# Two edits at the tail of a convolution and attention kernel: the store of the last sample but one in three parts, and one product of the last sample moved behind the attention's products

## What is computed

```python
im = relu(x); mn = mean(im); p = clip(u.T @ (im - mn), -cv, cv)
q  = round((p - dmin) * scale) / scale + dmin      # dmin, dmax over all samples
y  = u @ q - mean(u @ q) + mn
```

```python
h = relu(bn(w_conv1 @ y)); d = relu(bn(w_dr @ h + b_dr))
cov = covariance of d over the 3136 pixels of the sample     # 128 x 128
r = rows of cov weighted with w_row, plus b_row
att = sigmoid(w_fc @ r + b_fc)
out = y * att
```

## Time and profile before

| what | value |
|---|---|
| time, median of 3 runs | 1894.13 us (1892.45 to 1895.07) |
| time of the profiled execution | 1892.99 us |
| its span | 1891.2 us |
| PE busy | 1672.6 us (88%) |
| DVE busy | 1536.7 us (81%) |
| ACT busy | 1488.9 us (79%) |
| DMA, mean over the span | 252 GB/s |

### The profile page before, as it was taken

The page is one execution under the profiler, slowest core; times in us unless marked ns, Lnnn a source line. Parts: engine busy times, 40 slices in busy tenths (PEclk is TensorE's granted clock), DMA queues, the critical chain, the costliest instruction groups (busy, mean ns, idle before and its releaser), DMA issues.

```text
span 1891.2 us, 39996 instructions
## 1 busy us (share of the span) xinstructions
PE 1672.6 (88%) x13394; PEld 1316.9 (70%) x13394; DVE 1536.7 (81%) x2813; ACT 1488.9 (79%) x2265; POOL 460.3 (24%) x136
## 2 busy tenths in 40 slices
PE   8999999999992000589999999999999999999998
PEld 8999999999992000366666666666666766766665
DVE  6888888888887755667888888888888888888885
ACT  7777777777769997678888878878888787887885
POOL 7888888888860000000000000000000000000000
PEclk9999999999995555799999999999999999999999
DMA  9998999999999999402545546546455464554635
GB/s 336 371 374 307 375 356 325 370 341 342 373 350 399 429 430 430 169 1 90 207 168 186 204 164 221 171 172 222 158 214 183 155 237 160 199 191 162 233 115 205
DMA packets 140590, 477.36 MB, mean 252 GB/s; under 512 B 10624, under 2 KB 33536, under 8 KB 125568
## 3 DMA queue, kind: packets, MB, share of 16 engines
q1 hardware_dynamic: 140544, 476.75, 68.4%
HBM read 284.04 MB, written 192.68 MB: 252 GB/s over the span
## 4 chain that ended last, share of the span: by engine, by line
PE 56%; ACT 1%; DVE 1%; issue 1%; ACTq 0%; DVEq 0%
PE z_ps L970 18%; PE y_ps L944 17%; PE d_ps L897 14%; PE cov_ps L879 5%; PE ch_ps L955 1%; ACT h L1020 0%; PE ch_ps L910 0%; PE ch_ps L909 0%; ACT hh L1025 0%; DVE g L1185 0%; PE y_ps L926 0%; PE cov_ps L882 0%; DVE hl L1167 0%; PE z_ps L926 0%; PE d_ps L926 0%
## 5 line engine op out<-in xcount | busy, mean ns | idle before, releaser
L299 POOL TENSOR_TENSOR xl<-early,xh 128x1568 fp32r<-128x1568 f32 x128 | 459.4, 3590 | 96.6 <-ACT xh L258 96.6
L1167 DVE TENSOR_TENSOR hl<-h,hh 128x1024 f16<-128x1024 f32 (+2 forms) x224 | 244.1, 1090 | 100.6 <-ACT hh L1025 100.4
L970 PE MATMUL z_ps<-qr,wl 128*128 128x512 f16 (+2 forms) x896 | 315.1, 355 | 0.0
L970 PE MATMUL z_ps<-qr,wh 128*128 128x512 f16 (+2 forms) x896 | 314.9, 355 | 0.0
L944 PE MATMUL y_ps<-qr,udh 128*128 128x512 f16 x868 | 303.7, 353 | 1.8 <-ACT p_res L1054 1.8
L258 ACT ACTIVATE xh<-early 128x1568 fp32r<-128x1568 f32 x128 | 194.1, 1517 | 139.4 <-PE pp L316 139.3
L944 PE MATMUL y_ps<-qr,udl 128*128 128x512 f16 x868 | 303.2, 353 | 0.0
L1054 ACT ACTIVATE p_res<-y_ps,att_cy 128x512 f32<-128x512 f32 x434 | 288.0, 712 | 5.9 <-ACT att_cy L1038 4.3
L1020 ACT ACTIVATE h<-z_ps,sb_h 128x512 f32<-128x512 f32 (+2 forms) x448 | 264.1, 626 | 22.8 <-PE z_ps L970 19.9
L897 PE MATMUL d_ps<-vh,hh 128*128 128x128 f16 x1600 | 280.7, 220 | 1.4 <-DVE hl L1167 1.3
L897 PE MATMUL d_ps<-vh,hl 128*128 128x128 f16 x1600 | 280.7, 220 | 0.0
(11 more groups left out here) (190 smaller groups left out, 2852.6 us busy)
## 6 DMA issues: line engine op xcount, KB each, us to landing
early<-in_x_dram SPq DMA_DIRECT2D x128, 784.0 KB, 6.9
out_dram<-p_res SPq DMA_DIRECT2D x31, 3136.0 KB, 10.2
early<-p_scratch SPq DMA_DIRECT2D x42, 1568.0 KB, 12.7
p_res<-p_scratch SPq DMA_DIRECT2D x112, 512.0 KB, 4.2
p_scratch<-early SPq DMA_DIRECT2D x56, 784.0 KB, 7.8
p_scratch<-late SPq DMA_DIRECT2D x56, 784.0 KB, 7.8
p_res<-p_scratch SPq DMA_DIRECT2D x56, 384.0 KB, 3.2
late_tile<-p_scratch SPq DMA_DIRECT2D x13, 1568.0 KB, 12.8
```

The source lines that it names most:

```text
L299: nc.gpsimd.tensor_tensor(xl[:, k % 2], xs[:, k], xh[:, k % 2].bitcast(F32), ALU.subtract).then_inc(split_done, 1)
L970: last = nc.tensor.matmul(z_ps[:, m, 0:w], part[:, k, m * P:(m + 1) * P], qr[:, a, k, columns(s)], start=k == 0 and part is wh, stop=k == ...
L1167: nc.vector.tensor_tensor(hl[:, par, :, 0:w], h32[:, par, :, 0:w], hh[:, par, :, 0:w], ALU.subtract).then_inc(h_split, 1)
```

## The change

Two edits. SP no longer stores sample N-2 in step 4 of phase N. It issues three stores after the phases instead, of chunks 0 to 2, chunks 3 and 4, and chunks 5 and 6, each as soon as its chunks are in `yo`; SP's program has nothing else between its last earlier store and these, so that only the waits inside `store` decide when each one goes. The final wait on `out_stored[0]` counts the three.

On PE, the last sample's chunk 2 (`final_output(FINAL + 2, 2)`) is taken out of the group of three ahead of `logits`, and is made right behind `logits`. Chunks 0 and 1 stay ahead of it.

```diff
-                        if s == Y_LAG and exists(r2, a, back=2) and exists(r2, a, back=1):
+                        if s == Y_LAG and exists(r2, a, back=2) and exists(r2, a):
                             store(2 * r2 + a - 2, a, 0, CH)
 
                 phases(sp, phase)
 
+                parts_before = [(0, 3), (3, 5), (5, CH)]
+                for first, end in parts_before:
+                    store(N - 2, 0, first, end)
                 last_parts = [(c, c + 1) for c in range(CH)]
                 for first, end in last_parts:
                     store(N - 1, 1, first, end)
-                sp.wait_ge(out_stored[0], 16 * (N // 2) + 16)
+                sp.wait_ge(out_stored[0], 16 * (N // 2 - 1 + len(parts_before)) + 16)
...
-                            for n in range(0, 3) if c == 0 else range(c + 2, min(c + 3, CH)):
+                            for n in range(0, 2) if c == 0 else range(c + 2, min(c + 3, CH)):
                                 final_output(FINAL + n, n)
...
                         logits(r2, a, s)
+                        if s == Y_LAG and has(r2, a, s, CH + Y_LAG) and final(output_chunk(r2, a, s)[0]):
+                            final_output(FINAL + 2, 2)
                         reduced(r2, a, s)
```

## The result

The changed kernel took 1887.72 us in the median of 10 runs (1885.87 to 1888.41), the kernel before 1892.19 us in the 10 runs that go with them (1890.24 to 1895.07). The ratio is 0.9973, 95% interval 0.9964 to 0.9983: 5.1 us faster by the ratio, 4.5 by the medians. Two more comparisons of the same two kernels, of 11 against 33 runs each, gave 0.9982 (0.9973 to 0.9991) and 0.9981 (0.9972 to 0.9990), about 3.5 us. So the change makes the kernel faster, by 3.4 to 5.1 us in the three ratios.

A forecast was written before the change was run, and what follows sets the result against it. The end was bound by a DMA queue on one lagging engine. TensorE's chain 3.4, the lagging engine 1.8, less 0.8 for the stores' common queue, gave 4.4 us: 1894.13 - 4.4 = 1889.8 us, range 1888.0 to 1892.2.

The forecast's parts named there:

- The 20 us before as one engine's queue: Tail before: stores queued on one lagging DMA engine, 1871.7 + 0.9 + 8.0 + 1.9 + 8.0 + 0.7 = 1891.2 us.
- Size of the lag: One DMA engine at 1872.5 to 1875.0: an instruction packet's recorded time, 1.9 us, taken as its lag.
- Edit 1: Sample N-2's store split in three: early parts use idle DMA time, the lag no longer counts; 1.8 us gained alone.
- Rival (e): From 1862.5 to 1871.2: stores beside the attention chain slow it, at worst to 1898.4 us; chance 0.03.
- Edit 2: Chunk 2 behind the attention's products in the tail: everything behind moves up 1.73 us, plus 1.85 us from the clock.
- The clock: TensorE's chunks 3 and 4: without the 1.83 us idle stretch the granted clock stays at 1.00, saving 1.85 us.
- Rival (a): TensorE's tail: the clock falls all the same, so gain 3.4 us, time 1890.7; chance 0.10.
- The queue that takes over: Last sample's stores: 3.21 MB at about 400 GB/s takes 8.0 us and bounds the end, giving back 0.8 us.
- Rival (b): Last seven stores: an engine lags again, gain 2.5 to 3.5 us, time around 1891.3; chance 0.12.
- Rival (c): Tail: the 1.9 us lag is peculiar to the profiled execution, so gain 2.6 us, time 1891.5; chance 0.08.
- Rival (d): Tail: stores hardly go earlier or the end hangs on something else; gain 0 to 1, about 1893.6; chance 0.05.
- the step from the difference to the absolute time: Whole kernel: the 4.4 us gain taken from the shown runs' median, 1894.13 - 4.4 = 1889.8 us.

The follow-up runs named there:

- edit 2 alone: The kernel before with only chunk 2 moved behind the attention's products, sample N-2 stored whole; 1890.67 us against 1891.3, ratio 0.9998.
- packet moved: The kernel before plus 70 unread semaphore increments on TensorE, which shift its instruction fetch earlier; 1889.06 us against 1891.3, ratio 0.9989.
- the gap filled: Three stores of sample N-2, old chunk 2 order, plus seven unread matmuls behind the attention's products, against the kernel before; 1889.55 us against 1891.91, ratio 0.9986.
- edit 1 alone: The kernel before with only sample N-2's store split in three, chunk 2 still ahead of the attention's products; 1888.61 us against 1891.3, ratio 0.9987.
- the attention earlier: The changed kernel with the attention's products moved ahead of chunk 1's second half; 1886.95 us against the kernel before's 1891.91, ratio 0.9975.

## Why the prediction came out as it did

**The 20 us before as one engine's queue:** right. Undoing the lag in either of two ways, by earlier stores or by a moved packet, gives 18.2 us both times, and moving TensorE's chain alone gives 19.9. **Size of the lag:** 1.9 us before, as read. But I took the packet's own recorded time for the lag, and that is not right in general. With edit 2 alone the instruction queue's packet is recorded with

```profile
q8 instruction: 1, 0.02, 1.5%
```

over 4 us, 0.015 x 16 x 4 = 1.0 us, and the engine is 2.1 us late all the same. The packets in the traces show what the rest is made of. The first microsecond of the whole store, with edit 2 alone (1872.1 to 1873.1) and then with the packet moved (1873.0 to 1874.0):

```profile
q1 hardware_dynamic: 30, 0.38, 87.8%
```

```profile
q1 hardware_dynamic: 32, 0.40, 93.6%
```

Where the packet is out of the way, 16 engines take two packets of the store each. With edit 2 alone only 15 do: the sixteenth takes none from 1872.3 on, although the instruction packet is recorded only from 1873.12 to 1874.07. Its first store packet starts at 1874.06, where the instruction packet ends, and takes 0.86 us in place of the 0.47 of the others. That is 1.7 us of waiting and 0.4 us of a slow packet, together the 2.1. In the kernel before, the packet runs from 1872.75 to 1874.65, about as soon as the store begins, and 15 of 16 engines (share 0.95) carry the store meanwhile:

```profile
1872.80:1874.60 1.80, 1.80 (x10) 0.80 (x9) 0.93 (x2) 0.00 (x0) 0.00 (x0) 1.00 0.95 404
```

Its engine starts at 1874.63, again with a packet of 0.86 us. So it fell behind by 1.9 + 0.4 us, and the other 15 lost some 0.4 us while they waited for the last sample's chunks (share 0.61 from 1886.0 to 1886.7): from the store's begin to their end they need 15.9 us, with edit 2 alone 15.5. That the lag came out as long as the packet's record is luck: two terms of 0.4 us, both missing from the prediction's sum, cancel. Why the sixteenth engine takes nothing in the 0.8 us ahead of the recorded packet, and why its first store packet is slow, stays open.

The Trainium skill, DMA: Bandwidth & Descriptors, section Queues, rings and completion order, has each engine take turns between the queues that have work for it; its section Why a DMA increments its semaphore by 16 and not by 1 has a DMA complete only when all its engines have posted. The single engine's tail agrees with the second: the last store landed only when that engine was done. The traces agree with the first in that the late engine's stores went on when the instruction packet was over; turns alone don't give the 0.8 us.

**Edit 1:** right, 1.8 us alone, and the traffic beside the attention chain cost nothing. From the chain's chunk 3 of sample N-2 to the last sample's first product it is 1871.19 - 1862.88 = 8.31 us before and 1870.53 - 1862.23 = 8.30 after. Rival (e) falls.

**Edit 2:** right. DVE's last eviction begins 11.4 us behind the last sample's first product, against 1886.03 - 1871.19 = 14.8 before: 3.4 us earlier, as summed, 1.73 of it by the order and 1.7 by the clock (1.85 was said at first, with chunk 3 at 1.73 us; at full clock it took 1.90). **The clock:** right, with the gap filled as the test: after 1.83 us idle it fell to 0.50 in all three profiles that have the gap (before, edit 1 alone, packet moved), after 0.3 us or less in none of the other seven. Rival (a) falls.

**The queue that takes over:** right. From the first store's issue to the end it is 1886.2 - 1876.4 = 9.8 us, as summed; 1886.9 - 1877.1 = 9.8 with the gap filled, and 9.8 (1883.7 - 1873.9) with the attention earlier. Its rate was 403 GB/s, so the 358 GB/s that the Trainium skill, DMA: Bandwidth & Descriptors, section Specifications, gives for one core's HBM traffic does not hold here either, with one core at work. Rival (b), a lag among the last stores, was not met in the changed kernel's three profiles, and the two-part store shows how narrow that is: 1.4 MB more in the last part bring it back. What spoke for (b), the engine left over at the end of the store of 1848.89 us, has an instruction packet in it as well (from 1849.5 to 1858.4 us):

```profile
q14 instruction: 1, 0.01, 0.2%
```

It is recorded with 0.31 us at 1852.92, and only 15 engines carry the store in that time; this one was not moved as a test. Rival (c), a lag only in the profiled execution, is unlikely: the timed runs of edit 1 alone gain 2.5 us, those with the packet moved 2.1. Rival (d) falls with the three profiles of the changed kernel, all with a tail of 15.7 us in place of 20.0.

**What failed** is the step from the difference to the absolute time: "The median of the runs shown is 1894.13, 1.1 above it; I take the difference from there". The mis-sized term is that base. It was taken from three runs, with "the medians' own scatter of some 0.7". It measured 1892.19 in the ten runs of the result, of which those three are part (the other seven have a median of 1891.80), and 1891.3 and 1891.91 in the next two comparisons, 1.9 to 2.8 us lower. The measured 1892.19 - 4.4 would have been 1887.8, against 1887.72; the forecast of 1889.8 (its sum gives 1889.7) stood on a base 1.9 us too high, and the low end of 1888.0 lay 1.8 us under it. The start of the tail alone scatters by 3.7 us between executions, and the shown runs themselves, 1892.45 to 1895.07, would have told that a scatter of some us is there. It is a term mis-sized, not a mechanism missed. The 3.8 us that "a measurement of this kernel can't tell from no change" was too wide: the intervals reach 0.0009 or 0.0010 to each side, 1.7 to 1.9 us, so 3.4 us could be told. For 4.4 us against a bound of 3.8 the chance of 0.50 was fair: two of the three comparisons lie below that bound and one above.

## What to carry to other kernels

When stores run without a break to the end of a kernel, add up the queue of each DMA engine from the last time that it was idle. A lag of one engine in that stretch, here from one packet of instructions, stayed to the end, and a share of 0.06 after the others have stopped is its mark. Work that can be stored early should be, so that the last burst starts on idle engines.

Two bounds that lie close together hide each other: by the tails edit 2 alone was worth 0.2 us, and after edit 1 it was worth 2.5. Test such edits together as well as apart. And take an absolute forecast from the scatter of the whole kernel, not from the certainty of the part that changes.

## What the hardware showed that was not expected

A packet of 0.02 MB of instructions made one DMA engine 1.4 to 2.1 us late under a full queue of stores, where the record of the packet itself was 1.0 to 1.9 us; in an idle stretch (packet moved) it cost nothing. The engine took no store from the begin of the store to the end of the packet, so the record alone tells too little. The Trainium skill, Runtime: NRT & Kernel Launch, section Instruction fetch mechanics, says that instructions come in 16 KiB blocks over a DMA queue and that this is mostly hidden. It was hidden from TensorE here, which was busy for 1.80 of the 1.80 us from 1872.8 to 1874.6 while the packet came in; the stores that shared the engine paid.

SP's issues of the last sample's seven stores took different times in different kernels. With edit 2 alone, where all of sample N-2 is stored just ahead of them, six of the seven took 1.0 to 1.3 us. With sample N-2 in two parts four took 0.42 to 0.50 us and one 0.40. In the changed kernel all seven took 0.37, in the kernel before all but one, which took 0.57. That a backlog of stores holds up the issue would fit, but was not tested.
